# An adaLN attention and mixture-of-experts block on one core: the expert pick split in four, gate sums in the prologue, and four send, fetch and normalisation times moved

## The reference, cut to what matters

```
h = layernorm(x) * (1 + ca) + sa                      # sa, ca, ga, sb, cb, gb from silu(c) @ wmod
q, k, v = split(h @ w_attn)                           # 16 heads of 8; one k and one v
att = softmax(where(causal, q k^T / sqrt(8), -inf))
x = x + ga * ((att v) @ w_proj)                       # ga = sign(ga) * max(|ga|, 0.25); gb likewise
h = layernorm(x) * (1 + cb) + sb
g = sigmoid(h @ gate_w.T)                             # 16 experts
topv, topi = top_k(g, 4); share = topv / sum(topv)
routed = sum over e of share_e * ((silu(h @ e_win) * (h @ e_vin)) @ e_wout)
shared = (silu(h @ ws_in) * (h @ vs_in)) @ ws_out
x = x + gb * (shared + routed)
```

## Time and profile before

| | us |
|---|---|
| runs | 428.33, 428.38, 431.05 |
| median | 428.38 |
| the profiled execution's own time | 431.06 |
| its span, first to last instruction | 429.3 |
| busy: TensorE, VectorE, ScalarE, GpSimd | 375.5, 278.8, 228.4, 91.7 |
| mean granted clock of TensorE | 0.944 |
| chain that ended last: TensorE, VectorE, GpSimd | 57%, 21%, 8% |
| GpSimd's seven gate operations | 49.01 to 56.28 |
| GpSimd's norm of chunk 3 | 160.83 to 165.43 |
| TensorE idle, waiting for vin products on VectorE, at 160.4 and at 167.4 | 0.66 and 1.07 |
| pick of chunk 2 on VectorE | 167.90 to 172.33 |
| the combine rows of chunk 1 landed, and GpSimd's gate products began | 319.91 |
| the same chunk's rows, issue to landing, least, median, most of eight | 6.3, 8.9, 12.7 |

### The profile page before, as it was taken

One profiled execution on the slowest core, in us unless ns is written; L12 is line 12 of the kernel. 1 busy time (PEld: TensorE's weight loads), 2 busy tenths in 40 slices (PEclk: granted clock), 3 DMA queues, 4 the chain that ended last, 5 costly groups with the idle time before them and its releaser, 6 DMA issues.

```text
span 429.3 us, 6042 instructions
## 1 busy us (share of the span) xinstructions
PE 375.5 (87%) x2123; PEld 182.3 (42%) x2123; DVE 278.8 (65%) x649; ACT 228.4 (53%) x425; POOL 91.7 (21%) x123
## 2 busy tenths in 40 slices
PE   8598939879999996899989998998897999888984
PEld 7284513343346333343364433343542443235453
DVE  4579933797995887687537744897578892141464
ACT  2312517545668862454477545676584543679422
POOL 6120461080410069050054000005017000010000
PEclk9877779988999999799999999999998999899999
DMA  7361751403200900040900000000260000003200
GB/s 190 51 80 24 156 136 19 51 9 75 51 24 5 194 6 0 14 48 17 197 0 25 2 1 0 27 2 1 64 136 2 1 2 0 25 2 98 52 2 24
DMA packets 23773, 19.46 MB, mean 45 GB/s; under 512 B 6768, under 2 KB 20496, under 8 KB 23744
## 3 DMA queue, kind: packets, MB, share of 16 engines
q1 hardware_dynamic: 23328, 18.69, 21.6%
q10 hardware_dynamic: 416, 0.39, 0.3%
HBM read 11.22 MB, written 1.17 MB: 29 GB/s over the span
## 4 chain that ended last, share of the span: by engine, by line
PE 57%; DVE 21%; POOL 8%; issue 6%; ACT 6%; DMA 1%; SPq 0%; POOLq 0%; DVEq 0%; ACTq 0%
PE bank L942 53%; DVE mn L831 12%; ACT pr L681 2%; POOL xn L558 2%; POOL rstd L549 1%; ACT L681 1%; PE bank L1118 1%; DMA qa<-qp 1%; POOL sl L623 1%; PE bank L979 1%; DVE xn L758 1%; DVE stat L863 1%; ACT L685 1%; ACT sl L685 1%; DVE ka L817 1%
## 5 line engine op out<-in xcount | busy, mean ns | idle before, releaser
L831 DVE TENSOR_REDUCE mn<-bank 128x1 f32<-128x512 f32 (+3 forms) x304 | 185.7, 655 | 59.6 <-PE bank L942 59.2
L681 ACT ACTIVATE pr<-bank 128x512 f32<-128x512 f32 x288 | 160.8, 599 | 100.5 <-PE bank L942 98.4
L942 PE MATMUL bank<-ka,qa 96*128 96x128 bf16 (+3 forms) x576 | 111.9, 287 | 19.8 <-DVE mn L831 11.0
L942 PE MATMUL bank<-qa,ka 98*128 98x512 bf16 x288 | 111.1, 398 | 2.4 <-ACT pr L681 1.7
L942 PE MATMUL bank<-pr,va 128*32 128x512 f32 x576 | 80.5, 632 | 0.7 <-ACT pr L681 0.7
L942 PEld LDWEIGHTS bank<-ka,qa 96*128 96x128 bf16 x576 | 49.7, 102 | 69.3 <-DVE mn L831 33.7
L942 PEld LDWEIGHTS bank<-qa,ka 98*128 98x128 bf16 x288 | 28.5, 101 | 86.6 <-ACT pr L681 44.6
L942 PE MATMUL bank<-hT_parts,up_parts 128*128 128x512 f32 (+1 forms) x216 | 61.4, 412 | 1.9 <-DVE sl L932 1.1
L942 PEld LDWEIGHTS bank<-hT_parts,up_parts 128*128 128x128 f32 x216 | 38.5, 190 | 13.5 <-issue 3.1
L548 POOL TENSOR_SCALAR rstd<-mv 128x4 f32<-128x4 f32 (+2 forms) x9 | 2.1, 235 | 184.5 <-DVE mv L864 184.3
L623 POOL TENSOR_TENSOR sl<-sl,comb_wide 128x512 f32<-128x512 f32 x24 | 29.8, 1272 | 50.2 <-ACT sl L685 27.4
(11 more groups left out here) (140 smaller groups left out, 276.1 us busy)
## 6 DMA issues: line engine op xcount, KB each, us to landing
comb_wide<-comb_rows SPq DMA_DIRECT2D x6, 1024.0 KB, 10.1
qa<-q_marks SPq DMA_DIRECT2D x4, 768.0 KB, 5.7
qa<-qp SPq DMA_DIRECT2D x18, 128.0 KB
comb_wide<-comb_rows SPq DMA_DIRECT2D x2, 768.0 KB, 7.7
xs<-in_L_attn_x SPq DMA_DIRECT2D x4, 256.0 KB, 5.7
qa<-qp SPq DMA_DIRECT2D x12, 64.0 KB
out_x<-xs SPq DMA_DIRECT2D x3, 256.0 KB, 2.3
sl<-in_L_ffn_e_win SPq DMA_DIRECT2D x1, 512.0 KB, 7.7
```

The lines of the kernel that those rows point to most:

```text
L681: act.activation(pr[:, n % NPB, g, :], s_bank[in_s[x] % NS][:, :], ACT.Exp, scale=SCALE).then_inc(s_read, 1)
L831: v.tensor_reduce(mn[:, place[u] % 2, part, h:h + n], m_bank[k % NM][:, 0:n * w].rearrange("p (n w) -> p n w", w=w), AX.X, ALU.max, negate ...
L942: return pe.matmul(out, lhsT, rhs, start=start, stop=stop, skip_group_check=True)
```

## The change

- "gates" leaves the planner's queue and stands in the prologue, behind k_mid of chunk 2 and ahead of the maxima of unit 1.
- The marks of chunk 2 go from 4.0 to 0.2, its six sends from 1.5 + 2.5i to 0.5 + 1.3i, the fetch from 13.0 to 18.0, the weight splits from 34, 38, 41 to 28, 31, 34, and the normalisation of chunk 3 from 90 to 116.
- "pick" is in four parts, 0.8 of planner time apart, with the same instructions in the same order. combT follows the last part by 1.4 (before: the whole by 3.2).
- `through_shift` first ends a down projection that is under way and emits its "gated", and then the shift.

```diff
@@ -128,13 +128,15 @@
                             vins.append((now, ("vin", LAST, f)))
                         else:
                             plan.append(("down", LAST, f - 1))
-            plan.extend([("up_end", 0), ("pick", a), *(("up_end", i) for i in range(1, EP))])
+            plan.extend([("up_end", 0), *(("pick", a, i) for i in range(4)), *(("up_end", i) for i in range(1, EP))])
             plan.extend([("down", LAST, FC), ("gated", LAST), ("turn_end", 0), ("turn", LAST)])
             plan.extend([*(("turn_end", i) for i in range(1, ET)), ("down_end",)])
         elif kind == "route":
-            side.append((now + 1.4, ("pick", a)))
+            side.append((now + 1.4, ("pick", a, 0)))
+        elif kind == "pick" and x[2] < 3:
+            side.append((now + 0.8, ("pick", a, x[2] + 1)))
         elif kind == "pick":
-            smalls.append((now + 3.2, ("combT", a)))
+            smalls.append((now + 1.4, ("combT", a)))
         elif kind == "combT":
             side.append((now + 3.6, ("spread", a)))
         elif kind == "norm":
@@ -228,14 +230,18 @@
     plan += [("q_send", c0, n, s0, CH // 2) for s0 in (0, CH // 2) for n in SENDS]
     plan += [("k", c0), ("k_rest", c0), ("k_mid", c0), ("v", c0), ("k_set", c0)]
     side += [(4.0, ("stats", CHUNKS[2])), (6.0, ("stats", CHUNKS[3]))]
-    smalls += [(5.0, ("gates",))]
-    side += [(8.0, ("norm", CHUNKS[2])), (90.0, ("norm", CHUNKS[3])), (4.0, ("marks", c1)), (13.0, ("fetch",)), (34.0, ("w_split", 0)),
-             (38.0, ("w_split", 1)), (41.0, ("w_split", 2)), (44.0, ("marks", CHUNKS[2])), (60.0, ("marks", CHUNKS[3])), (10.0, ("sentinels",))]
+    side += [(8.0, ("norm", CHUNKS[2])), (116.0, ("norm", CHUNKS[3])), (0.2, ("marks", c1)), (18.0, ("fetch",)), (28.0, ("w_split", 0)),
+             (31.0, ("w_split", 1)), (34.0, ("w_split", 2)), (44.0, ("marks", CHUNKS[2])), (60.0, ("marks", CHUNKS[3])), (10.0, ("sentinels",))]
 
     def through_shift(u):
         while st["job"] <= last_job[u]:
             one_max()
         while ("shift", u) not in plan:
+            while st["down"]:
+                others()
+            for x in [x for x in side if x[1][0] == "gated"]:
+                side.remove(x)
+                emit(x[1])
             x = next(x for x in smalls if x[1] == ("shift", u))
             smalls.remove(x)
             emit(x[1])
@@ -246,13 +252,13 @@
 
     plan += [("loads",), ("hT", c1), ("q", c1), ("q_rest", c1)]
     max_of(order[0])
-    plan += [("k", c1), ("k_rest", c1), ("k_mid", c1)]
+    plan += [("k", c1), ("k_rest", c1), ("k_mid", c1), ("gates",)]
     while st["job"] <= last_job[order[1]]:
         one_max()
         plan.append(("fill", 2))
     plan += [("v", c1)]
     through_shift(order[0])
-    side.extend((1.5 + 2.5 * i, ("q_send", c1, n, 0, CH)) for i, n in enumerate(SENDS))
+    side.extend((0.5 + 1.3 * i, ("q_send", c1, n, 0, CH)) for i, n in enumerate(SENDS))
     for j in range(6):
         one_max()
     plan += [("k_set", c1)]
@@ -871,27 +877,31 @@
                     own(v.tensor_copy(hT_parts[:, k, 0, 0:w], whole))
                     v.tensor_tensor(hT_parts[:, k, 1, 0:w], whole, hT_parts[:, k, 0, 0:w], ALU.subtract).then_inc(h2_last, 1)
                 elif kind == "pick":
-                    c = x[1]
+                    c, part = x[1:]
                     us, n = units(c), group[c][2]
-                    r = ("route", c)
-                    v.wait_ge(small_read[at[r]], use[r] + 1)
-                    v.wait_ge(sent_ready, 1)
-                    own(v.tensor_scalar(eg[:, us, 0:E], eg[:, us, 0:E], 1.0, None, ALU.add))
-                    own(v.reciprocal(eg[:, us, 0:E], eg[:, us, 0:E]))
-                    for i in range(n):
-                        steps[0] += 1
-                        v.max(top[:, i, :], eg[:, us.start + i, 0:E]).then_inc(dve, 1)
-                    v.wait_ge(dve, steps[0])
-                    own(v.tensor_copy(top[:, 0:n, TOPK:8], eg[:, us, E:SENT]))
-                    for i in range(n):
-                        steps[0] += 1
-                        v.match_replace(out=rest[:, i, :], in_to_replace=top[:, i, :], in_values=eg[:, us.start + i, :],
-                                        imm_value=0.0).then_inc(dve, 1)
-                    own(v.tensor_reduce(tsum[:, 0, 0:n], top[:, 0:n, 0:TOPK], AX.X, ALU.add))
-                    own(v.reciprocal(tsum[:, 1, 0:n], tsum[:, 0, 0:n]))
-                    own(v.tensor_tensor(rest[:, 0:n, 0:E], eg[:, us, 0:E], rest[:, 0:n, 0:E], ALU.subtract))
-                    v.tensor_tensor(eg[:, us, 0:E], rest[:, 0:n, 0:E], tsum[:, 1, 0:n].unsqueeze(2).broadcast_to([P, n, E]),
-                                    ALU.mult).then_inc(share_ready, 1)
+                    if part == 0:
+                        r = ("route", c)
+                        v.wait_ge(small_read[at[r]], use[r] + 1)
+                        v.wait_ge(sent_ready, 1)
+                        own(v.tensor_scalar(eg[:, us, 0:E], eg[:, us, 0:E], 1.0, None, ALU.add))
+                        own(v.reciprocal(eg[:, us, 0:E], eg[:, us, 0:E]))
+                    elif part == 1:
+                        for i in range(n):
+                            steps[0] += 1
+                            v.max(top[:, i, :], eg[:, us.start + i, 0:E]).then_inc(dve, 1)
+                        v.wait_ge(dve, steps[0])
+                        own(v.tensor_copy(top[:, 0:n, TOPK:8], eg[:, us, E:SENT]))
+                    elif part == 2:
+                        for i in range(n):
+                            steps[0] += 1
+                            v.match_replace(out=rest[:, i, :], in_to_replace=top[:, i, :], in_values=eg[:, us.start + i, :],
+                                            imm_value=0.0).then_inc(dve, 1)
+                        own(v.tensor_reduce(tsum[:, 0, 0:n], top[:, 0:n, 0:TOPK], AX.X, ALU.add))
+                    else:
+                        own(v.reciprocal(tsum[:, 1, 0:n], tsum[:, 0, 0:n]))
+                        own(v.tensor_tensor(rest[:, 0:n, 0:E], eg[:, us, 0:E], rest[:, 0:n, 0:E], ALU.subtract))
+                        v.tensor_tensor(eg[:, us, 0:E], rest[:, 0:n, 0:E],
+                                        tsum[:, 1, 0:n].unsqueeze(2).broadcast_to([P, n, E]), ALU.mult).then_inc(share_ready, 1)
                 elif kind == "gate" and x[1] == LAST:
                     c, f = x[1:]
                     v.wait_ge(comb_in[c], 32)
```

## The result

| | before | after |
|---|---|---|
| runs, side by side | 428.33, 428.38, 431.05, 434.74 | 423.25, 423.66, 424.29, 426.12 |
| median | 429.72 | 423.98 |
| ratio of after to before, 95% interval | | 0.9867 [0.9827, 0.9907] |
| span of the profiled execution | 429.3 | 424.4 |
| busy: TensorE, VectorE, GpSimd | 375.5, 278.8, 91.7 | 377.8, 273.5, 92.2 |

What follows compares the result with a forecast made beforehand. TensorE, busy 375.5 of 429.3 us and partly at half clock, was the bound. Terms: -5.0 (A, B), -2.5 (C), -6.0 and -2.0 (D), -2.5 - 2.2 + 5.0 + 1.0 + 1.2 (E): -13.0 from 428.38, say 415; range 407 to 425.

Steps and rivals of the forecast that it cites:

- A: Chunk 2's first maximum: earlier query sends ahead of the fetch end a TensorE wait (-4.65) and the half clock after (-1.7).
- B: Gate sums in the prologue: projection wait and copies go (-2.2, -1.1), gate_w wait and slowed shift operations come (+3.6, +1.0): +1.3.
- C: Earlier weight splits on GpSimd no longer slow VectorE's key copies of chunk 1, and less half clock follows: -2.5 us.
- D in chunk 2: Pick in four and chunk 3's normalisation moved ahead of chunk 2's gates: less TensorE idle and half clock, -6.0 us.
- E3: Shift 7 held behind down projection 2, so TensorE waits for its transfer (+3.5) and a half-clock spell follows (+1.5): +5.0.
- E4: k_set of chunk 3 comes to lie beside gate products of chunk 2: +1.0 us (0 to 2.5).
- D in chunk 1: Pick of chunk 1 in four parts reduces TensorE's 2.86 us idle there: -2.0 us.
- E1: Later combT of chunk 1 keeps GpSimd's gates off three shift operations at 322: -2.5 us.
- E2: Shift 15 precedes down projection 1 and needn't wait for its evacuation: idle and the clock after it go, -2.2 us.
- E5: Tail: pick parts stand between hidden-layer products, so combT comes later: +1.2 us (0 to 3).
- R1: Rival, chance 0.20: the stall only moves, VectorE being the near bound from 150 to 190; 420 to 425, middle 422.
- R2 to R4: Rivals: every half-clock spell goes, 406 (chance 0.13); no change within 1%, 428 (0.07); slower, chunk 3's queries late (0.05).

Runs made afterwards that it cites:

- e9: Kernel after with the normalisation of chunk 3 at 90 again and the load of gate_w ahead of SP's whole plan: 415.42 us, ratio to before 0.9655.
- e3: Kernel after with the four parts of each pick directly behind one another and combT due 3.2 later: 423.53 us, ratio to before 0.9861.
- e4: Kernel after with down projection 2 held back behind shift 7, normalisation of chunk 3 left at 116: 419.92 us, ratio to before 0.9761.
- g3: Kernel before with only the pick in four parts, combT 1.4 after it, and through_shift finishing a down projection in hand: 423.15 us, ratio 0.9759.
- e8: Kernel after with down projection 2 held behind shift 7 and gate_w loaded ahead of SP's plan: 417.78 us, ratio to before 0.9698.

## Why the prediction was right or wrong

- **A, -4.65 and -1.7: right in what happened, wrong as a term of its own.** The sends stand ahead of the fetch and the wait is gone. The sixth went at 53.27 and not 47.5, since the prologue's delay (B) moved the shift in front of it from 44.04 to 51.06; TensorE came to chunk 2's first maximum only after 61, so this cost nothing. But A was priced as though nothing else ended near it. The gate sums and, behind them on GpSimd, chunk 1's normalisation did. The latter is in no step of the prediction.
- **B, +1.3.** The wait for w_projg went. Unit 1's shift came 5.7 us later, against +4.6 in the step: gate_w took 8.3 us to land and not 6.4, and the products behind the wait ran at half clock (0.50 from 26 to 34; in the kernel before 1.00 from 28). The +1.0 for shift operations beside GpSimd didn't come in this execution (they stand at 39.6, GpSimd ended at 39.5); in e9 one did: 0.74 for 0.17, beside an operation of 0.72 that had begun 0.02 us earlier. A and B together gave -3.0 in the profile, -3.1 by groups of kernels, not -5.0; with the early load -5.4. Of this B alone, on top of A, was -0.3 (47.2 against 47.5), and not +1.3.
- **C, -2.5: right, if anything too small.** The splits fitted in front of k_mid, and the copies took 0.28. The profile of after shows -0.8, with a spell of 7 us at half clock in the stage that e3 and e4, in the same order up to there, don't have (23.9 and 23.8); by the kernels it's -3.5, and -2 by the timed ratio. VectorE waited near 85 for TensorE alone (1.6 at most), not for a split or k_mid.
- **D in chunk 2, -6.0: the step that failed.** It credited the pick's parts and the moved normalisation together with the idle time and the half clock at 168 to 178. The parts alone took the 4.36 down to 1.36 (g3, e9), with the normalisation at 90. In stage IV they give -3.1: 132.0 against 135.1 in four kernels with the whole pick. That is their idle time alone. The half clock that the step counted as won came here all the same, after a wait of 1.71 in the kernel after, and the stage's mean clock is 0.97 with and without the parts. GpSimd's normalisation between two gate products, which looked like the cause by the earlier trace rows, had nothing to give. So the step's reason for moving the normalisation failed: the move was to bring a part of these 6.0 us, brought nothing, and cost 6.4 (next point).
- **E3, +5.0, and E4, +1.0.** E3 was the step "I'm least sure of", and it's right in kind: 1.35 + 2.32 of idle and half clock behind, 3.5 us by e4 and e8 in place of 5.0. What is left of the move, 2.9 us, was forecast as 1.0: chunk 3 is now prepared just ahead of unit 7, and TensorE waits more there, on VectorE above all (in e8 9.0 us of waits in stage IV, in e9 7.3; the last us of the 2.9 no run places). So the move costs 6.4 us in all, close to the 6.0 that E3 and E4 gave it. The sum for stage IV, with these sizes, is -3.1 + 3.5 + 2.9 = +3.3; forecast was 0, measured +4.4 in one profile and +3.3 by groups. This stage makes more than half of the 8 us that the profile is above the forecast; the rest is A with B (+2.0), C (+1.7) and a later start (+1.4), less the tail (-1.5).
- **D in chunk 1, E1, E2, -6.7: right** (-6.5, and -5.6 over all kernels). 2.86 became 0.81; the shift operations of unit 14 took 0.17 each; shift 15 waited for nothing, though 1.82 moved to a transpose at 367.83, 16 us behind its own. By how much the parts and the later combT each did this isn't shown.
- **E5, +1.2:** not seen, the tail is 0.3 shorter.
- **The rivals.** The time came out where R1 had put it (420 to 425), but not by R1's mechanism: stalls didn't just move to a busy VectorE, C and E1 gave what they were to give. The pick in parts pays 8 to 10 us, A to C together 6.6 (47.2 + 25.3 against 50.3 + 28.8 in I and II, by groups of kernels), and the moved normalisation takes 6.4 back. These sizes add up to some -9, and -5.7 was measured. What makes the difference isn't shown: half-clock spells that fall into one execution and not the next may be it, and the kernel before itself stood at 430.9 to 432.3 in the rounds of experiments and at 429.7 in the first comparison. R2 to R4 didn't come; chunk 3's queries were in time. That the time lies in the stated range is in part luck: the range reached so high for R1's sake.
- **The mean clock** was to rise to 0.96 and fell to 0.936. It reached 0.955 only in e8 and e9. I priced each spell that a removed wait had caused as gone, and of those that would begin anew only the one at shift 7 (1.5).

Of the rule cited from the Trainium skill (SBUF — State Buffer, "SBUF: two separate sides"): the trace agrees, the 0.74 above ends when GpSimd's operation ends, while row maxima, which read from a bank, kept their 0.69 beside GpSimd.

Still open: what A alone is worth at the end of the kernel. It saves 3.7 us of TensorE's idle time in stage I, and its ten timed runs are 0.5 us below before, with some 1.6 us of doubt. Its profile places the rest in a lower clock later on, which can be chance; no run tells whether it would come again.

## What to carry to other kernels

When several edits are made around one wait, look at what ends next behind it on each engine's queue, not only on the one that is waited for: an edit may be worth next to nothing alone and 8 us in company, and its partner alone may be a loss. Cut long blocks on the engine that frees the banks before moving other work about, and credit a stall to the cheapest edit that would end it, once. Before a step is moved by more than its own length, follow by hand what its new place pushes in front of a step with a date (here down projection 2 ahead of shift 7): a due time moved by 26 of the planner's units undid more than half of the gain.
